# Splitting the weights on the engine that subtracts, and loading two of them through a second staging tile

## The chip, the cores and the metric

The kernel runs as one program on all 8 cores of one Trainium2 chip. Each core takes its own 4096 tokens with 256 tokens of warm-up in front (4352 tokens, 17 tiles of 256); there is no traffic between cores. The metric is device time in microseconds (us) of the slowest core.

## The reference

One layer of a "sandwich": a gated linear attention and a gated feed-forward network, each between two layer norms and added to its input.

```python
x = x + LN(attn(LN(x)));  x = x + LN(ffn(LN(x)))      # x: (2, 16384, 1024) f32
# attn: q = silu(x Wq^T); f = sigmoid(x Wk^T); g = log_sigmoid(f); k = 1 - f; v = x Wv^T
#       S = exp(g_t) S + k_t v_t^T ; o_t = q_t S (8 heads of 128) ; out = rmsnorm(o) * norm_w @ Wo^T
# ffn:  xr, xk = mixes of x and its predecessor in time by mu_r, mu_k
#       out = sigmoid(xr Wr^T) * (relu(xk Wk2^T)^2 Wv2^T)
```

## The kernel before

Activations lie transposed: 1024 features as 8 groups of 128 partitions, 256 tokens along the free dimension, so a tile is 128 x 2048 f32. Every f32 operand of a large product is split into a bf16 high part and a bf16 rest (`_h`, `_l`), and each product is three bf16 matmuls (high·high, high·rest, rest·high) added up in PSUM. `proj_feature` (L241) does this for one group of 128 output features: 24 matmuls into one of the two banks `p_pj`, after which another engine must empty the bank before the next but one group starts.

Phase A (before L690) holds Wk, Wq and Wv split in SBUF, runs the attention for 17 tiles and stores its result in the DRAM tensor `o_scr`. Phase B then takes the same SBUF for Wo, Wr, Wk2 and Wv2 and runs, tile by tile, the output projection and the feed-forward part.

Each weight comes in through `load_split_weight` (L166): 8 rounds, one for each 128 rows. In a round SP issues a 512 KB DMA into the one staging tile `wstage` (L172), ScalarE (ACT) copies it to bf16 (L180), and VectorE (DVE) or GpSimd (POOL) subtracts that high part from the f32 value into the rest (L183). The next DMA waits for the subtraction, as there is one staging tile; Wo has a scaling by `norm_w` on DVE ahead of the copy (L176). So nothing overlaps within a weight, and the weights of a phase follow each other.

The order between the phases is that of the program text, engine by engine: the DMAs of tile 0 (`b_load_dma`), Wo's rounds, then tile 0's output projection (`b_load_wo`), its scaling (`b_aobc`), its residual (`b_x2`, which puts the load of the next `xB` into SP's queue, waiting for DVE), and its second norm and mixes (`b_ln2_xrxk`). Only then come the rounds of Wr, Wk2 and Wv2, then the DMA of `oB` for tile 1. Each loop turn `it` from 1 to 17 then does, for p = `it` and q = p - 1: `b_load_wo(p)`, `b_wr(q)`, `b_wk2(q)`, `b_wv2(q)`, `b_aobc(p)`, `b_ffstat(q)`, `b_fin(q)`, `b_x2(p)`, `b_ln2_xrxk(p)`. In `b_load_wo` ACT copies `oB` to the high part `o_h` (L759), POOL subtracts (L761), TensorE (PE) multiplies, and ACT empties each bank into `scr1` (L768); the first of these copies waits until the mixes of the tile before (`pv["xk"]`, DVE L935) have read `scr1`. The mixes of `b_ln2_xrxk` are a chain of DVE instructions from L912 to L935 that uses `scr2` from L921 on.

Each `bld.flush()` closes a block of instructions on every engine; there is one after each loop turn and between the stages above. ACT works with function tables; the instruction ACT_TABLE_LOAD is put in by the compiler and bears the line of the instruction behind it.

Of the kernel before, what the change touches and what calls it, by code (L numbers as in the profile page):

```python
# [8 lines left out]
AF = mybir.ActivationFunctionType  # L9
ALU = mybir.AluOpType  # L10

D = 1024
# [80 lines left out]
def build_program(tok, warm, debug=False):  # L93
# [30 lines left out]
    op, ev, C = bld.op, bld.ev, bld.cnt  # L124
# [30 lines left out]
    for dst, src in ((mask4, mask4v), (onesc, onescv), (onesr, onesrv),  # L155
                     (nw, nwv), (mur, murv), (muk, mukv)):
        op("sync", lambda e, dst=dst, src=src: e.dma_start(out=dst[:], in_=src),
           inc=[("LW", 16)])
# [4 lines left out]
    op("vector", lambda e: e.memset(eps5[:], EPS_LN), inc=[("V", 1)], nop=True)  # L163
    op("vector", lambda e: e.memset(eps6[:], EPS_RMS), inc=[("V", 1)], nop=True)

    def load_split_weight(src_ap, dst_h, dst_l, scale_nw=False, first_wait=(), eng="vector"):  # L166
        E = "V" if eng == "vector" else "G"
        srcc = src_ap.rearrange("(c p) n -> p c n", p=128)
        last = None
        for ci in range(NCH):  # L170
            wv = [(E, C[E])] + (list(first_wait) if ci == 0 else [])
            op("sync", lambda e, ci=ci, srcc=srcc: e.dma_start(  # L172
                out=wstage[:], in_=srcc[:, ci:ci + 1, :]), wait=wv, inc=[("LW", 16)])
            wl = [("LW", C["LW"]), ev_cdma]
            if scale_nw:
                op(eng, lambda e, ci=ci: e.tensor_scalar_mul(  # L176
                    wstage[:, 0, :], wstage[:, 0, :], nw[:, ci:ci + 1]),
                   wait=wl + [(E, C[E])], inc=[(E, 1)])
                wl = [(E, C[E])]
            ev_h = op("scalar", lambda e, dst_h=dst_h, ci=ci: e.activation(  # L180
                out=dst_h[:, ci, :], in_=wstage[:, 0, :], func=AF.Copy),
                wait=wl + [("S", C["S"])], inc=[("S", 1)])
            op(eng, lambda e, dst_h=dst_h, dst_l=dst_l, ci=ci: e.tensor_tensor(  # L183
                dst_l[:, ci:ci + 1, :], wstage[:], dst_h[:, ci:ci + 1, :], ALU.subtract),
               wait=[ev_h, (E, C[E])], inc=[(E, 1)])
            last = ev(E)
        return last

    state = {
        "bc_read": ("V", 0),  # L190
        "bc_ev": ("T", 0),
        "pj_free": [("V", 0), ("V", 0)],
        "stats_free": ("V", 0),
# [64 lines left out]
    for nm in ("wk", "wq", "wv"):  # L258
# [27 lines left out]
    Ax_h = ctxA.enter_context(nc.sbuf_tensor("Ax_h", [128, 2, 512], BF16))  # L286
    Ax_l = ctxA.enter_context(nc.sbuf_tensor("Ax_l", [128, 2, 512], BF16))

    ev_wk = load_split_weight(w_in["wkT"], wA["wkh"], wA["wkl"], eng="vector")
    ev_wq = load_split_weight(w_in["wqT"], wA["wqh"], wA["wql"], first_wait=[ev_wk],  # L290
                              eng="gpsimd")
    ev_wv = load_split_weight(w_in["wvT"], wA["wvh"], wA["wvl"], first_wait=[ev_wq],
                              eng="vector")
    bld.flush()

    st = {
# [454 lines left out]
    def b_load_wo(p):  # L751
        pv = bt[p - 1] if p > 0 else bt[nt]
        me = bt[p]
        if p > 0:
            b_load_dma(p)
        ev_o = ev("LO")
        ev_rrow = ev("LR")
        me["x_ld"] = ("LX", C["LX"])
        ev_oh = op("scalar", lambda e: e.activation(out=o_h, in_=oB[:], func=AF.Copy),  # L759
                   wait=[ev_o, pv["WoT"], pv["revac"], ("S", C["S"])], inc=[("S", 1)])  # L760
        op("gpsimd", lambda e: e.tensor_tensor(o_l, oB[:], o_h, ALU.subtract),  # L761
           wait=[ev_oh, ("G", C["G"])], inc=[("G", 1)])
        ev_ospl = ev("G")
        ev_aoev = None
        for dj in range(NCH):
            evt = proj_feature(wB["woh"], wB["wol"], o_h, o_l, dj,
                               extra_wait=[ev_ospl, ev_wo] if dj < 2 else [])
            ev_aoev = op("scalar", lambda e, dj=dj: e.activation(  # L768
                out=scr1[:, dj, :], in_=p_pj[dj % 2][:, 0:TILE], func=AF.Copy),
                wait=[evt, pv["xk"], ("S", C["S"])], inc=[("S", 1)])  # L770
            state["pj_free"][dj % 2] = ev_aoev
        me["WoT"] = ("T", C["T"])
        ev_sq = op("scalar", lambda e: e.activation(out=sqA, in_=scr1[:], func=AF.Square),
                   wait=[ev_aoev, ("LO", C["LO"]), state["stats_free"], ("S", C["S"])],
                   inc=[("S", 1)])
# [25 lines left out]

    def b_wk2(q):
        me = bt[q]
        ev_kev = None
        for dj in range(NCH):
            evt = proj_feature(wB["wk2h"], wB["wk2l"], xk_h, xk_l, dj,
                               extra_wait=[ev_wk2, me["xk"]] if dj < 2 else [])
            ev_kev = op("scalar", lambda e, dj=dj: e.activation(
                out=scr2[:, dj, :], in_=p_pj[dj % 2][:, 0:TILE], func=AF.Relu),
                wait=[evt, bt[q - 1]["ffstat"] if q > 0 else TZ, ("S", C["S"])]  # L810
                if dj == 0 else [evt],
                inc=[("S", 1)])
            state["pj_free"][dj % 2] = ev_kev
        ev_wk2T = ("T", C["T"])
        op("vector", lambda e: e.tensor_tensor(scr2[:], scr2[:], scr2[:], ALU.mult),
           wait=[ev_kev, ("V", C["V"])], inc=[("V", 1)])
        op("vector", lambda e: e.tensor_copy(kc_h[:], scr2[:]),
           wait=[("V", C["V"]), ev_wk2T], inc=[("V", 1)])
        op("vector", lambda e: e.tensor_tensor(kc_l[:], scr2[:], kc_h[:], ALU.subtract),  # L819
           wait=[("V", C["V"])], inc=[("V", 1)])  # L820
        me["kc"] = ev("V")
# [16 lines left out]
    def b_aobc(p):  # L838
        me = bt[p]
        bcast_rows()  # L840
        me["aobc"] = ("T", C["T"])
        op("vector", lambda e: e.tensor_tensor(scr1[:], scr1[:], bcA(), ALU.mult),
           wait=[me["aobc"], ("V", C["V"])], inc=[("V", 1)])
        op("vector", lambda e: e.tensor_tensor(scr1[:], scr1[:], bcB(), ALU.add),
           wait=[("V", C["V"])], inc=[("V", 1)])
        state["bc_read"] = ev("V")
# [44 lines left out]
    def b_ln2_xrxk(p):  # L891
# [23 lines left out]
        mur_bc = mur[:].unsqueeze(2).broadcast_to([128, NCH, TILE])  # L915
        muk_bc = muk[:].unsqueeze(2).broadcast_to([128, NCH, TILE])
        q = p - 1
        gate_scr2 = bt[q]["ffstat"] if q >= 0 else TZ
        gate_xr = bt[q]["WrT"] if q >= 0 else TZ
        gate_xk = bt[q]["Wv2T"] if q >= 0 else TZ  # L920
        op("vector", lambda e: e.tensor_tensor(scr2[:], scr1[:], mur_bc, ALU.mult),  # L921
# [14 lines left out]
           wait=[("V", C["V"])], inc=[("V", 1)])  # L936
        me["xk"] = ev("V")

    b_load_dma(0)
    ev_wo = load_split_weight(w_in["woT"], wB["woh"], wB["wol"], scale_nw=True,  # L940
                              first_wait=ev_A_drain, eng="vector")
    op("vector", lambda e: e.memset(ln2[:], 0.0), inc=[("V", 1)], nop=True)
    ev_ln2init = ev("V")
    b_load_wo(0)
    b_aobc(0)
    b_x2(0)
    b_ln2_xrxk(0)
    bld.flush()
    ev_wr = load_split_weight(w_in["wrT"], wB["wrh"], wB["wrl"], first_wait=[ev_wo],
                              eng="gpsimd")  # L950
    ev_wk2 = load_split_weight(w_in["wk2T"], wB["wk2h"], wB["wk2l"], first_wait=[ev_wr],
                               eng="vector")
    ev_wv2 = load_split_weight(w_in["wv2T"], wB["wv2h"], wB["wv2l"], first_wait=[ev_wk2],
                               eng="gpsimd")
    bld.flush()
    for it in range(1, nt + 1):
        p, q = it, it - 1
# [94 lines left out]
```

How the kernel before makes its waits and increments, by code:

```python
        def closure(e, fn=fn, waits=waits, incs=tuple(incs), nop=nop):  # L51
            for sem, v in waits:
                e.wait_ge(sem, v)
            if nop:
                e.engine_nop()
            ins = fn(e)
            for sem, k in incs:
                ins.then_inc(sem, k)
# [11 lines left out]
        def closure(e, waits=waits):  # L70
            for sem, v in waits:
                e.wait_ge(sem, v)
```

## Time and profile before

| | us |
|---|---|
| profiled execution, time | 5739.41 |
| profiled execution, span of the slowest core | 5737.9 |
| runs shown | 5741.77 and 6156.08, median 5948.93 |

| engine | busy us | share of the span |
|---|---|---|
| PE | 3483.3 | 61% |
| DVE | 1945.3 | 34% |
| ACT | 1153.0 | 20% |
| POOL | 478.6 | 8% |

The profile is one execution, taken on the slowest core. "Busy" is the time in instructions of an engine. A wait is shown as idle time ahead of an instruction with what released it. The chain that ended last is followed back from the last instruction, at each step to what released it. Of that chain 52% is PE, 27% DVE, 9% ACT, 5% DMA, 4% issue and 2% POOL.

### The profile page before, as it was taken

Reading aid. Unit: us, or ns where it says so; the run is one execution under the profiler, and the core shown is the slowest. Engines: PE = TensorE matmul, PEld = TensorE weight load, DVE = VectorE, ACT = ScalarE, POOL = GpSimd, SP = SyncE. Lnnn points to the kernel's source line nnn. Section 1 sums busy time; section 2 is a strip of 40 time slices with the busy share of each in tenths; the row PEclk is TensorE's granted clock in tenths of the full one; section 3 lists DMA queues with packets and bytes.
Section 4 is the critical chain, followed back from the end, with each engine's and each line's share of the span. In section 5 each row is a group of like instructions: output and inputs, shape, how many; then the busy total and the mean of one; then the engine's idle time right before and its main releaser. Section 6 shows DMA issues by size and latency. Waiting matters only on the chain.

```text
span 5737.9 us, 65929 instructions; the slowest of 8 cores (5727.0 to 5737.9 us)
## 1 busy us (share of the span) xinstructions
PE 3483.3 (61%) x26608; PEld 2616.6 (46%) x26608; DVE 1945.3 (34%) x1912; ACT 1153.0 (20%) x1672; POOL 478.6 (8%) x198
## 2 busy tenths in 40 slices
PE   0566666666666666662236666766566675656675
PEld 0344444444444444441134455544445554444554
DVE  1333333333333333333303323333433323333233
ACT  1222222222222222222111111111111111111110
POOL 1111111111111111111110000000000000000000
PEclk9877777777777777776667888878788887878887
DMA  2000000000000000001110000000000000000000
GB/s 78 26 15 15 15 15 15 15 15 15 15 15 16 15 15 15 15 8 52 52 52 15 23 23 8 15 23 23 23 23 23 8 16 23 23 23 23 23 8 8
DMA packets 69041, 121.85 MB, mean 21 GB/s; under 512 B 3683, under 2 KB 55046, under 8 KB 62214
## 3 DMA queue, kind: packets, MB, share of 16 engines
q1 hardware_dynamic: 68742, 117.63, 6.2%
q8 instruction: 216, 3.54, 0.3%
q14 instruction: 83, 0.68, 0.0%
HBM read 83.00 MB, written 34.62 MB: 20 GB/s over the span
## 4 chain that ended last, share of the span: by engine, by line
PE 52%; DVE 27%; ACT 9%; DMA 5%; issue 4%; POOL 2%; DVEq 1%; ACTq 0%; SPq 0%; POOLq 0%
PE p_pj L250 38%; PE p_st L231 4%; PE p_pj L402 4%; DVE b_sb L331 3%; DVE r_a L207 1%; PE p_O L516 1%; PE p_O L533 1%; DMA outT<-x_sb 1%; ACT ebq L363 1%; PE p_A L481 1%; PE p_bc L216 1%; DVE p_A L459 1%; DVE scr L912 1%; DVE A_l L464 1%; DVE A_h L462 1%
## 5 line engine op out<-in xcount | busy, mean ns | idle before, releaser
L250 PE MATMUL p_pj<-o_pair,woh 128*128 128x256 bf16 x2176 | 419.5, 300 | 516.8 <-POOL o_pair L761 333.3
L250 PEld LDWEIGHTS p_pj<-o_pair,woh 128*128 128x128 bf16 x2176 | 230.9, 107 | 576.6 <-issue 531.8
L231 PE MATMUL p_st<-x_sb,onesc 128*1 128x256 f32 x544 | 179.7, 503 | 485.9 <-ACT oB L894 275.6
L250 PE MATMUL p_pj<-ln_h,wkh 128*128 128x256 bf16 x1088 | 308.3, 283 | 199.6 <-DVE ln_l L614 199.6
L250 PE MATMUL p_pj<-xk_h,wv2h 128*128 128x256 bf16 x1088 | 311.2, 286 | 119.0 <-DVE xk_l L819 119.0
L231 PEld LDWEIGHTS p_st<-x_sb,onesc 128*1 128x1 f32 x544 | 54.6, 103 | 610.1 <-issue 584.2
L250 PE MATMUL p_pj<-o_pair,wol 128*128 128x256 bf16 x1088 | 325.0, 299 | 0.0
L250 PE MATMUL p_pj<-xr_h,wrh 128*128 128x256 bf16 x1088 | 297.6, 274 | 25.0 <-DVE xk_l L935 24.8
L250 PE MATMUL p_pj<-xk_l,wv2h 128*128 128x256 bf16 x1088 | 311.6, 286 | 0.0
L250 PE MATMUL p_pj<-ln_h,wqh 128*128 128x256 bf16 x1088 | 310.1, 285 | 2.5 <-ACT fq_sb L649 2.5
L250 PE MATMUL p_pj<-xk_h,wv2l 128*128 128x256 bf16 x1088 | 310.3, 285 | 0.0
L250 PE MATMUL p_pj<-ln_l,wqh 128*128 128x256 bf16 x1088 | 309.2, 284 | 0.0
L250 PE MATMUL p_pj<-ln_h,wql 128*128 128x256 bf16 x1088 | 308.8, 284 | 0.0
L250 PE MATMUL p_pj<-ln_l,wkh 128*128 128x256 bf16 x1088 | 308.8, 284 | 0.0
L250 PE MATMUL p_pj<-ln_h,wkl 128*128 128x256 bf16 x1088 | 307.7, 283 | 0.0
L250 PE MATMUL p_pj<-xr_l,wrh 128*128 128x256 bf16 x1088 | 297.5, 273 | 0.0
L250 PE MATMUL p_pj<-xr_h,wrl 128*128 128x256 bf16 x1088 | 297.5, 273 | 0.0
L250 PE MATMUL p_pj<-xk_l,wk2h 128*128 128x256 bf16 x1088 | 296.6, 273 | 0.0
L250 PE MATMUL p_pj<-xk_h,wk2l 128*128 128x256 bf16 x1088 | 296.6, 273 | 0.0
L250 PE MATMUL p_pj<-xk_h,wk2h 128*128 128x256 bf16 x1088 | 296.6, 273 | 0.0
L481 PE MATMUL p_A<-qt_h,kx_h 128*128 128x128 bf16 x264 | 71.5, 280 | 369.3 <-DVE A_l L464 369.3
L761 POOL TENSOR_TENSOR o_pair<-oB,o_pair 128x2048 bf16<-128x2048 f32 x17 | 69.1, 4065 | 2544.3 <-ACT o_pair L759 2544.3
(177 smaller groups left out, 7936.7 us busy)
## 6 DMA issues: line engine op xcount, KB each, us to landing
x_sb<-xT SPq DMA_DIRECT2D x17, 1024.0 KB, 5.0
o_scr<-o_stage SPq DMA_DIRECT2D x68, 256.0 KB, 2.3
oB<-o_scr SPq DMA_DIRECT2D x17, 1024.0 KB, 4.9
xB<-xT SPq DMA_DIRECT2D x17, 1024.0 KB, 5.0
outT<-x_sb SPq DMA_DIRECT2D x16, 1024.0 KB, 4.4
wstage<-wkT SPq DMA_DIRECT2D x8, 512.0 KB
wstage<-wqT SPq DMA_DIRECT2D x8, 512.0 KB
wstage<-wvT SPq DMA_DIRECT2D x8, 512.0 KB
```

The lines of the kernel that those rows point to most:

```text
L207: op("vector", lambda e: e.reciprocal(r_a[:], r_t0[:]), wait=[("S", C["S"])], inc=[("V", 1)], nop=True)
L216: op("tensor", lambda e: e.matmul(p_bc[:, 0:TILE], onesr[:], r_a[:], start=True, stop=False), wait=wv)
L231: op("tensor", lambda e, ci=ci: e.matmul(p_st[0:1, 0:TILE], onesc[:], x_ap[:, ci, :], start=(ci == 0), stop=(ci == NCH - 1)), wait=wv if c ...
L250: e.matmul(bank[:, 0:TILE], wop[:, ci, dj * 128:(dj + 1) * 128], xop[:, ci, :], start=first, stop=last),
L331: op("vector", lambda e, h=h, tsl=tsl: e.tensor_tensor_scan(b_sb[:, h, :], g_sb[:, h, tsl], g_sb[:, h, tsl], 0.0, ALU.add, ALU.bypass), wa ...
L363: op("scalar", lambda e, h=h: e.activation(out=ebq[:, h, :], in_=b_sb[:, h, :], func=AF.Exp, scale=-1.0, bias=b_sb[:, h, CH - 1:CH]), wait ...
L402: e.matmul(bank[:], lnop[:, ci, tsl], wop[:, ci, half * 512:(half + 1) * 512], start=first, stop=last),
L459: op("vector", lambda e, bank=bank: e.tensor_tensor(bank[:], bank[:], mask4[:], ALU.mult), wait=[ev_Amm[g4], ("V", C["V"])], inc=[("V", 1)])
L462: op("vector", lambda e, bank=bank, Ah=Ah: e.tensor_copy(Ah[:], bank[:]), wait=[("V", C["V"])], inc=[("V", 1)])
L464: op("vector", lambda e, bank=bank, Ah=Ah, Al=Al: e.tensor_tensor(Al[:], bank[:], Ah[:], ALU.subtract), wait=[("V", C["V"])], inc=[("V", 1)])
L481: e.matmul(bank[:, (h - 4 * g4) * 128:(h - 4 * g4 + 1) * 128], kop[:, xpar, h, :], qop[:, h, :], start=first, stop=last),
L761: op("gpsimd", lambda e: e.tensor_tensor(o_l, oB[:], o_h, ALU.subtract), wait=[ev_oh, ("G", C["G"])], inc=[("G", 1)])
```

## The change

`load_split_weight` lets DVE or POOL itself make the bf16 copy that ACT made, and gets a staging tile and a semaphore as arguments. Wr and Wv2 are staged in the first half of `scr2` instead of `wstage`, split by POOL, and their 16 rounds stand ahead of tile 0's `b_aobc`, `b_x2` and `b_ln2_xrxk` in the program; the users of `scr2` wait for them (`scr2_ld`). Wk2 stays behind tile 0's mixes, through `wstage`, split by DVE. In `b_load_wo` the copy to `o_h` moves from ACT to POOL, for all 17 tiles.

```diff
@@ load_split_weight(..., stage=None, lsem="LW")
+        wst = wstage[:] if stage is None else stage
-            op("sync", ... dma_start(out=wstage[:], ...), wait=wv, inc=[("LW", 16)])
+            op("sync", ... dma_start(out=wst, ...), wait=wv, inc=[(lsem, 16)])
-            ev_h = op("scalar", lambda e, dst_h=dst_h, ci=ci: e.activation(
-                out=dst_h[:, ci, :], in_=wstage[:, 0, :], func=AF.Copy),
-                wait=wl + [("S", C["S"])], inc=[("S", 1)])
-            op(eng, ... e.tensor_tensor(
-                dst_l[:, ci:ci + 1, :], wstage[:], dst_h[:, ci:ci + 1, :], ALU.subtract),
-               wait=[ev_h, (E, C[E])], inc=[(E, 1)])
+            op(eng, lambda e, dst_h=dst_h, ci=ci, wst=wst: e.tensor_copy(
+                dst_h[:, ci:ci + 1, :], wst), wait=wl + [(E, C[E])], inc=[(E, 1)])
+            op(eng, ... e.tensor_tensor(
+                dst_l[:, ci:ci + 1, :], wst, dst_h[:, ci:ci + 1, :], ALU.subtract),
+               wait=[(E, C[E])], inc=[(E, 1)])
@@ b_load_wo
-        ev_oh = op("scalar", lambda e: e.activation(out=o_h, in_=oB[:], func=AF.Copy),
-                   wait=[ev_o, pv["WoT"], pv["revac"], ("S", C["S"])], inc=[("S", 1)])
+        op("gpsimd", lambda e: e.tensor_copy(o_h, oB[:]),
+           wait=[ev_o, pv["WoT"], pv["revac"], ("G", C["G"])], inc=[("G", 1)])
         op("gpsimd", lambda e: e.tensor_tensor(o_l, oB[:], o_h, ALU.subtract),
-           wait=[ev_oh, ("G", C["G"])], inc=[("G", 1)])
+           wait=[("G", C["G"])], inc=[("G", 1)])
@@ b_wk2, b_ln2_xrxk (tile 0's first writer of scr2)
-   ... else TZ
+   ... else state["scr2_ld"]
@@ between the phases
+    sview = scr2[:].rearrange("p a b -> p (a b)")[:, 0:D].unsqueeze(1)
     b_load_dma(0)
     ev_wo = load_split_weight(w_in["woT"], ..., scale_nw=True,
-                              first_wait=ev_A_drain, eng="vector")
+                              first_wait=ev_A_drain, eng="vector", lsem="SW")
     ...
     b_load_wo(0)
+    ev_wr = load_split_weight(w_in["wrT"], ..., first_wait=ev_A_drain,
+                              eng="gpsimd", stage=sview, lsem="LB")
+    ev_wv2 = load_split_weight(w_in["wv2T"], ..., first_wait=[ev_wr],
+                               eng="gpsimd", stage=sview, lsem="LB")
+    state["scr2_ld"] = ev_wv2
     b_aobc(0)
     b_x2(0)
     b_ln2_xrxk(0)
     bld.flush()
-    ev_wr = load_split_weight(..., first_wait=[ev_wo], eng="gpsimd")
-    ev_wk2 = load_split_weight(..., first_wait=[ev_wr], eng="vector")
-    ev_wv2 = load_split_weight(..., first_wait=[ev_wk2], eng="gpsimd")
+    ev_wk2 = load_split_weight(w_in["wk2T"], ..., first_wait=[ev_wo],
+                               eng="vector", lsem="SW")
```

Wk, Wq and Wv keep their order and `wstage`; their loads count on another semaphore.

## Rows read from the trace of the kernel before

**Rows 1.** Busy by windows, weight stretch: us, PE, PEld, DVE, ACT, POOL, PEclk, DMA, GB/s.
```profile
2800.00:2957.00 157.00, 0.00 (x0) 0.00 (x0) 27.43 (x16) 26.43 (x24) 36.41 (x15) 0.50 0.25 79
```

**Rows 2.** Chain that ended last, first weights: start us, length us, what.
```profile
16.25 1.06 ACT wkh L180
17.48 1.24 DVE wkl L183
...
22.50 1.06 ACT wkh L180
...
66.93 1.06 ACT wqh L180
68.19 2.13 POOL wql L183
...
74.12 1.06 ACT wqh L180
```

**Rows 3.** The same chain between the two phases.
```profile
2717.22 3.51 DMA wstage<-woT
...
2942.45 6.84 DMA oB<-o_scr
...
2957.17 23.24 PE p_pj L250 x192
```

**Rows 4.** Timeline of SP's queue between the phases: start, length, what.
```profile
2774.79 61.43 SPq L172 DMA_DIRECT2D wstage<-wrT  x8
2842.85 43.48 SPq L172 DMA_DIRECT2D wstage<-wk2T  x8
2892.54 49.71 SPq L172 DMA_DIRECT2D wstage<-wv2T  x8
```

**Rows 5.** Groups by line and shape: xcount | busy us, mean ns | idle before.
```profile
L183 DVE TENSOR_TENSOR wkl<-wstage,wkh 128x1024 bf16<-128x1024 f32 x8 | 9.8, 1225 | 44.9 <-ACT wkh L180 44.9
...
L817 DVE CAST xk_h<-scr 128x2048 bf16<-128x2048 f32 x17 | 20.8, 1226 | 2.9 <-DVE scr L815 2.9
...
L912 DVE TENSOR_TENSOR scr<-ln 128x2048 f32<-128x2048 f32 x17 | 52.0, 3060 | 1.8
...
L638 POOL TENSOR_SCALAR k_sb<-fq_sb 128x2048 f32<-128x2048 f32 x17 | 32.3, 1898 | 999.5 <-ACT fq_sb L627 999.5
...
L761 POOL TENSOR_TENSOR o_pair<-oB,o_pair 128x2048 bf16<-128x2048 f32 x17 | 69.1, 4065 | 2544.3 <-ACT o_pair L759 2544.3
```

**Rows 6.** The same view, ACT's table loads.
```profile
L759 ACT ACT_TABLE_LOAD x16 | 20.5, 1283 | 44.3 <-DMA oB<-o_scr 44.3
...
L180 ACT ACT_TABLE_LOAD x3 | 3.8, 1283 | 22.4 <-DVE wstage L176 13.5 <-DMA wstage<-wkT 8.8
```

**Rows 7.** Timeline of one later tile: POOL, then DVE, then ACT.
```profile
3436.05 4.07 POOL L761 TENSOR_TENSOR o_pair<-oB,o_pair 128x2048 bf16<-128x2048 f32 x1 [163.38 <-ACT o_pair L759]
...
3438.99 3.27 DVE L912 TENSOR_TENSOR scr<-ln 128x2048 f32<-128x2048 f32 x1
3442.51 2.29 DVE L921 TENSOR_TENSOR scr<-scr,mur 128x2048 f32<-128x2048 f32 x1 [0.24 <-DVE scr L912]
...
3457.29 2.29 DVE L935 TENSOR_TENSOR xk_l<-scr,xk_h 128x2048 bf16<-128x2048 f32 x1
...
3432.64 1.28 ACT L759 ACT_TABLE_LOAD   x1 [2.91 <-DMA oB<-o_scr]
...
3459.73 0.86 ACT L768 ACTIVATE scr<-p_pj 128x256 f32<-128x256 f32 x2 [23.88 <-DVE xk_l L935]
```

**Rows 8.** ACT's timeline around a table load.
```profile
3321.20 0.51 ACT L789 ACTIVATE r_msq<-r_var,eps 1x256 f32<-1x256 f32 x1 [8.25 <-DVE r_var L787]
3321.78 1.28 ACT L728 ACT_TABLE_LOAD   x1
3323.07 0.38 ACT L728 ACTIVATE r_sb<-p_pj 128x256 f32<-128x256 f32 x1
```

**Rows 9.** Waits, whole span: us in total, times, longest.
```profile
PE p_pj L250 <- ACT scr L768: 183.5, 15, 13.3
```

More of the change, by code:

```diff
@@ L164, in build_program, with load_split_weight @@
     op("vector", lambda e: e.memset(eps6[:], EPS_RMS), inc=[("V", 1)], nop=True)
-    def load_split_weight(src_ap, dst_h, dst_l, scale_nw=False, first_wait=(), eng="vector"):
+    def load_split_weight(src_ap, dst_h, dst_l, scale_nw=False, first_wait=(), eng="vector",
+                          stage=None, lsem="LW"):
         E = "V" if eng == "vector" else "G"
+        wst = wstage[:] if stage is None else stage
         srcc = src_ap.rearrange("(c p) n -> p c n", p=128)
@@ L171, in load_split_weight @@
             wv = [(E, C[E])] + (list(first_wait) if ci == 0 else [])
-            op("sync", lambda e, ci=ci, srcc=srcc: e.dma_start(
-                out=wstage[:], in_=srcc[:, ci:ci + 1, :]), wait=wv, inc=[("LW", 16)])
-            wl = [("LW", C["LW"]), ev_cdma]
+            op("sync", lambda e, ci=ci, srcc=srcc, wst=wst: e.dma_start(
+                out=wst, in_=srcc[:, ci:ci + 1, :]), wait=wv, inc=[(lsem, 16)])
+            wl = [(lsem, C[lsem]), ev_cdma]
             if scale_nw:
-                op(eng, lambda e, ci=ci: e.tensor_scalar_mul(
-                    wstage[:, 0, :], wstage[:, 0, :], nw[:, ci:ci + 1]),
+                op(eng, lambda e, ci=ci, wst=wst: e.tensor_scalar_mul(
+                    wst[:, 0, :], wst[:, 0, :], nw[:, ci:ci + 1]),
                    wait=wl + [(E, C[E])], inc=[(E, 1)])
                 wl = [(E, C[E])]
-            ev_h = op("scalar", lambda e, dst_h=dst_h, ci=ci: e.activation(
-                out=dst_h[:, ci, :], in_=wstage[:, 0, :], func=AF.Copy),
-                wait=wl + [("S", C["S"])], inc=[("S", 1)])
-            op(eng, lambda e, dst_h=dst_h, dst_l=dst_l, ci=ci: e.tensor_tensor(
-                dst_l[:, ci:ci + 1, :], wstage[:], dst_h[:, ci:ci + 1, :], ALU.subtract),
-               wait=[ev_h, (E, C[E])], inc=[(E, 1)])
+            op(eng, lambda e, dst_h=dst_h, ci=ci, wst=wst: e.tensor_copy(
+                dst_h[:, ci:ci + 1, :], wst), wait=wl + [(E, C[E])], inc=[(E, 1)])
+            op(eng, lambda e, dst_h=dst_h, dst_l=dst_l, ci=ci, wst=wst: e.tensor_tensor(
+                dst_l[:, ci:ci + 1, :], wst, dst_h[:, ci:ci + 1, :], ALU.subtract),
+               wait=[(E, C[E])], inc=[(E, 1)])
             last = ev(E)
@@ L190, in build_program @@
         "bc_read": ("V", 0),
+        "scr2_ld": ("G", 0),
         "bc_ev": ("T", 0),
@@ L287, in build_program @@
     Ax_l = ctxA.enter_context(nc.sbuf_tensor("Ax_l", [128, 2, 512], BF16))
-    ev_wk = load_split_weight(w_in["wkT"], wA["wkh"], wA["wkl"], eng="vector")
+    ev_wk = load_split_weight(w_in["wkT"], wA["wkh"], wA["wkl"], eng="vector",
+                              lsem="TT")
     ev_wq = load_split_weight(w_in["wqT"], wA["wqh"], wA["wql"], first_wait=[ev_wk],
-                              eng="gpsimd")
+                              eng="gpsimd", lsem="TT")
     ev_wv = load_split_weight(w_in["wvT"], wA["wvh"], wA["wvl"], first_wait=[ev_wq],
-                              eng="vector")
+                              eng="vector", lsem="TT")
     bld.flush()
@@ L809, in b_wk2 @@
                 out=scr2[:, dj, :], in_=p_pj[dj % 2][:, 0:TILE], func=AF.Relu),
-                wait=[evt, bt[q - 1]["ffstat"] if q > 0 else TZ, ("S", C["S"])]
+                wait=[evt, bt[q - 1]["ffstat"] if q > 0 else state["scr2_ld"],
+                      ("S", C["S"])]
                 if dj == 0 else [evt],
@@ L917, in b_ln2_xrxk @@
         q = p - 1
-        gate_scr2 = bt[q]["ffstat"] if q >= 0 else TZ
+        gate_scr2 = bt[q]["ffstat"] if q >= 0 else state["scr2_ld"]
         gate_xr = bt[q]["WrT"] if q >= 0 else TZ
@@ L944, in build_program @@
     b_load_wo(0)
+    ev_wr = load_split_weight(w_in["wrT"], wB["wrh"], wB["wrl"], first_wait=ev_A_drain,
+                              eng="gpsimd", stage=sview, lsem="LB")
+    ev_wv2 = load_split_weight(w_in["wv2T"], wB["wv2h"], wB["wv2l"], first_wait=[ev_wr],
+                               eng="gpsimd", stage=sview, lsem="LB")
+    state["scr2_ld"] = ev_wv2
     b_aobc(0)
@@ L948, in build_program @@
     bld.flush()
[L949 to L954, printed above, removed]
+    ev_wk2 = load_split_weight(w_in["wk2T"], wB["wk2h"], wB["wk2l"], first_wait=[ev_wo],
+                               eng="vector", lsem="SW")
     bld.flush()
```

## The prediction, made before the changed kernel was seen

> **What bounds the kernel now.** I read the busy shares of the page first (PE is highest at 61%, so waits matter), then the chain that ended last, then the windows in which PE does nothing. PE stands still in two stretches: the first 157 us, and the one between the phases, where in 157 us it has no instruction at all and its granted clock is 0.50 [rows 1]. Both are weight loads. The chain shows a round's structure: copy on ACT, subtraction, DMA, copy, one after the other. From copy to copy a DVE round is 22.50 - 16.25 = 6.25 us and a POOL round 74.12 - 66.93 = 7.19 us [rows 2]. SP's queue gives the same for the later weights: seven periods of Wk2 in 43.48 - 0.33 (the last issue) is 6.16 us each, Wv2 7.05, and Wr 8.73, since tile 0's DVE chain runs beside it [rows 4]. PE starts tile 1 at 2957.17, at the end of wv2's last round, then oB's DMA, ACT's copy and POOL's subtraction [rows 3]. In the later tiles the end is set by a serial loop in which the DVE mixes count: ACT's first copy out of PSUM waits for L935 and PE waits for ACT [rows 7], in 15 tiles [rows 9].
>
> **A round.** On DVE the ACT copy and its hand-over (17.48 - 16.25 = 1.23 us [rows 2]) give way to a DVE copy of 128x1024. That form isn't in the trace; the subtraction at 1024 takes 1.23 and at 2048 2.29 [rows 5, 7], so about 0.16 is fixed, and the copy of 2048 with 1.23 [rows 5] gives 0.16 + 1.07/2 = 0.69, at most the subtraction's 1.23. With a hand-over of 0.10 that is 0.79: 0.44 saved in each round. On POOL 1.26 us (68.19 - 66.93 [rows 2]) give way to a POOL copy. The nearest rows are one-input POOL work on 2048 (L638, 1.90) and the two-input subtraction (4.07 for 2048 [rows 5], 2.13 for 1024 [rows 2]), fixed part about 0.18. Half of L638's rest is 0.86 + 0.18 = 1.04 as the likely value, since the copy reads one input as L638 does; the dear end is 2.13, the cheap end the DVE's 0.69. With a hand-over of 0.15 a POOL round goes from 7.19 to 7.12: nothing gained. The Trainium skill (GPSIMD Engine Reference, Engine selection) puts one-input GpSimd work at roughly line rate and two-input work at about twice the DVE's time; the two rows agree with both.
>
> **The first weights.** Wk and Wv: 16 x 0.44 = 7.0. Wq: 8 x 0.07 = 0.6. ACT's first table load of 1.28 [rows 6] goes from the path: DVE starts at once. Together -8.9 us, with no cover over it, since nothing else runs.
>
> **Between the phases.** In the times of before, without those 8.9 us:
> - Wo's eighth issue was at 2717.22 [rows 3]. It comes 1.28 (table load, one of the three at L180 [rows 6]) and 7 x 0.44 = 3.1 earlier, and about 2 later, because POOL now splits tile 0's oB while Wo's first rounds need DVE: 2714.8. That POOL and DVE get in each other's way is in the trace: L912 takes 3.27 instead of 2.29 where POOL's L761 is still running, and its end at 3442.26 is POOL's end 3440.12 plus nearly its own 2.29 [rows 7].
> - PE's Wo(0) now follows Wo's last subtraction directly, as oB was split meanwhile. That chain no longer sets the end: tile 0's mixes will wait at L921 for scr2.
> - Wr's first DMA is issued 0.5 later in SP's queue (its waits, POOL's split and the drain of phase A, are over) and lands after 3.5 plus 1 for sharing with Wo's: 2719.8. Sixteen POOL rounds: the first 3.3 without its DMA, fifteen of 7.12 are 106.8: 2829.9. Collisions with DVE cost Wr's seven periods 61.43 - 49.71 = 11.7 us [rows 4] under the whole chain of mixes; now only x2 and L912 and small row work meet them: +3, so 2833.
> - Behind Wv2 waits DVE's L921, and behind it the mixes: from 3442.51 to 3459.58 is 17.1 us [rows 7]: 2850. Wk2's DMAs wait for their end; xB's load stands ahead of them in SP's queue but was released long before. Seven periods of 6.16 - 0.44 = 5.72 are 40.0: eighth issue 2890. oB's DMA follows 0.5 later and lands after 6.84 [rows 3]: 2897.5. POOL copy 1.90 and subtraction 4.07 with hand-overs of 0.5: PE starts tile 1 at 2904, where it was 2957.2. That is -53 us.
>
> **The later tiles.** ACT loses L759, which isn't on the path: PE does two groups after it and then stands until 3459.73, so an earlier Wo start is worth nothing. Two things around it count.
> - POOL starts about where ACT's table load started, 3432.64 [rows 7]: + 0.1 + 1.90 + 0.15 + 4.07 = 3438.86, just before L912 at 3438.99. L912's excess is 52.0 - 17 x 2.29 = 13.1 us over all tiles [rows 5]: -12. With a POOL copy at 4.07 it would be 15 x 1.1 = 16 dearer instead.
> - The table load doesn't vanish. ACT loads one in each of the 16 turns that begin with L759 [rows 6], after the wait of that instruction (the DMA), also with Sqrt already done before, while L789's Sqrt behind the Copy needs none: each block of instructions begins without a known table. L759 was the first ACT instruction of its block; now it is L768, whose wait is for L935. So a load of 1.28 that lay under other work moves between DVE's mixes and PE: 15 x 1.28 = +19.2 us. In tiles 0 and 1 L768 waits for PE only, and PE has the other bank to fill: nothing.
>
> Around a load I count no more than its 1.28: L789 ends at 3321.71, the load begins at 3321.78 and the next ACTIVATE at 3323.07 [rows 8]. The Trainium skill (ScalarE: Activation LUTs, What ACT_TABLE_LOAD costs) adds a drain of about 1.38 us to each switch; by that page the move would cost 40 us and the estimate would end near 5705. No drain shows in the row.
>
> **Sum.** -8.9 - 53 - 12 + 19.2 = -54.7. The profiled execution took 5739.4 us, 0.04% below the lower of the two runs shown and 3.5% below their median, which lies between two far values. The forecast goes by the profiled execution: 5739.4 - 54.7 = 5684.7, taken as 5684.
>
> **The rivals.**
> 1. *The table load isn't exposed*: the compiler needs none ahead of the Copy, or puts it ahead of the wait. For it: only L768's place in a block is inferred. Against: all 16 loads of L759 come right behind its DMA wait. Then 5684 - 19 = 5665. The Trainium skill (ScalarE: Activation LUTs, Table sets) says that cheap functions are in every set, which speaks for this one; the load at L759, itself a Copy, speaks against it. Chance 0.13.
> 2. *The POOL copy costs as much as the subtraction*, 2.13 and 4.07. For it: nothing but that the form is unseen. Then 24 rounds on the path x 1.09 = 26, tile 1's split 2, and in the later tiles 16 + 12 = 28 more: 5740, no change. Chance 0.13.
> 3. *Slower than before*: a POOL copy of more than 2.1 us for 1024 elements per partition. From there each further us costs 24 for the weight rounds and 15 x 2 = 30 in L912's wait: at 3.1 us it is 5794, within 2% still. Against it is L638. Chance 0.03.
> 4. *The rounds between the phases overlap better or worse*: no collisions and a full cover give 5 us less, collisions as Wr had over all of tile 0's work 9 more, and a DVE copy without its double speed 32 x 0.54 = 17 more: 5679 to 5710. This is the range of the forecast itself, whose chance is 0.68. The last 0.03 is for what I don't see.
>
> So the likeliest case's own range is 5672 to 5710; with the rivals, 8 times in 10 it is 5660 to 5725. A measurement tells about 2% (115 us) from no change; all cases but the tails lie within it: faster 0.03, same 0.95, slower 0.02.
>
> **What would show it.** Right: weight rounds of 5.8 on DVE and 7.1 on POOL; a POOL copy of 1.9 at L759's place; L912 at 2.29; PE's first matmul of tile 1 about 62 us earlier (2895); a table load at L768 in 16 turns, in 15 of them between L935 and the copy. Wrong: a POOL copy above 1.5 for 1024, no load at L768, or PE starting tile 1 later than 2910, which would mean that the sixteen POOL rounds collide more than 3 us' worth.

## The result, and the profile after

The changed kernel is faster by 1.1%: the ratio of the times is 0.9894, with an interval of 0.9877 to 0.991. In microseconds that is 61 of 5740. Its profiled execution took 5669.09 us where that of before took 5739.41, so 70.3 less, and the forecast was 54.7 less. The other times of the changed kernel in the comparison go from 5668.4 to 5691.8, those of before from 5740.2 to 5741.8; the profiled execution lies near the low end of its own. In some executions of every kernel the cores of a die ran at a lower clock and longer; all times, stages and ratios below are of undisturbed executions or dies.

The cores of the changed kernel, with the granted clock:

```profile
die 0 (median of its cores): 5664.0 us, clock 0.806
die 1 (median of its cores): 5662.7 us, clock 0.806
```

To see where time went I cut each core's trace at four marks: SP's issue of the first `x_sb`, the first and the last store of `rms_scr` (one in each turn of phase A), and PE's first matmul of tile 1 in phase B. These are medians over the cores, in us; the last column is the core's whole span. Short labels are those of the experiments.

```
kernel        x_sb issued  to 1st store  loop A  between  loop B  core span
before            156.6        200.8     2299.2   297.8   2778.0   5731.8
after             149.8        199.9     2288.5   243.8   2782.1   5663.0
e1_copies         149.4        200.1     2291.9   285.7   2777.0   5705.8
e2_order          157.9        200.1     2285.6   311.6   2777.5   5735.7
e3_oh             157.0        201.8     2299.2   292.9   2786.8   5738.9
e4_delay1         164.2        200.1     2293.7   298.8   2781.0   5737.6
e6_hide           150.4        201.4     2285.1   243.4   2778.1   5659.9
e7_delay          157.7        199.9     2287.0   244.0   2786.2   5677.5
e9_oh_back        150.9        201.1     2286.8   246.2   2777.8   5663.6
e10_one           157.2        201.7     2298.9   298.2   2777.6   5734.1
e11_two           158.0        200.8     2299.2   297.1   2778.1   5733.7
e12_three         158.2        199.8     2299.2   297.1   2778.7   5732.8
```

In e7_delay cores 2 and 3 ran at a lower clock (0.801 beside 0.804 to 0.806) and their loop B took 2801 to 2802; its die 1 alone has 2784.0 there.

So -6.8 for the first weights, -54.0 between the phases, -10.7 in a loop whose code is the same, and +4.1 in loop B.

The chain that ended last, between the phases of the changed kernel (start, length, what), answers [rows 3]:

```profile
2641.54 8.47 DMA wstage<-woT
2650.24 2.86 DVE wstage L178
...
2696.62 4.15 DMA scr<-wrT
2702.24 2.93 POOL wrl L184
...
2813.18 2.30 DVE scr L925
...
2830.18 3.86 DMA wstage<-wk2T
...
2873.25 5.44 DMA oB<-o_scr
2880.97 4.07 POOL o_pair L764
2885.27 23.94 PE p_pj L252 x192
```

And SP's queue for the same stretch, to be held against [rows 4]:

```profile
2696.62 52.12 SPq L174 DMA_DIRECT2D scr<-wrT  x8
2755.45 50.95 SPq L174 DMA_DIRECT2D scr<-wv2T  x8
2806.51 0.37 SPq L892 DMA_DIRECT2D xB<-xT  x1
2830.18 42.87 SPq L174 DMA_DIRECT2D wstage<-wk2T  x8
2873.25 0.33 SPq L745 DMA_DIRECT2D oB<-o_scr  x1
```

The reader is to see the chain that was forecast. Sixteen POOL rounds follow each other without a hole, DVE's first mix on `scr2` starts as the last of them ends, Wk2 follows the mixes, then `oB`. PE starts tile 1 at 2885.27 instead of 2957.17, 71.9 earlier. The forecast of that point was 62 earlier; on these two cores 18.4 of the 71.9 are there before the last store of phase A's loop (7.7 from the start, 10.7 in the loop), and about 53.5 are gained between the phases.

The groups by line and shape, to be held against [rows 5]:

```profile
L182 DVE CAST wkh<-wstage 128x1024 bf16<-128x1024 f32 x8 | 5.6, 694 | 34.2 <-DMA wstage<-wkT 34.2
L182 POOL CAST wqh<-wstage 128x1024 bf16<-128x1024 f32 x8 | 8.3, 1036 | 81.7 <-DMA wstage<-wqT 81.7
L762 POOL CAST o_pair<-oB 128x2048 bf16<-128x2048 f32 x17 | 32.1, 1890 | 2518.3 <-DMA oB<-o_scr 2518.3
L916 DVE TENSOR_TENSOR scr<-ln 128x2048 f32<-128x2048 f32 x17 | 39.0, 2292 | 1.8
L771 ACT ACT_TABLE_LOAD x17 | 21.8, 1283 | 638.7 <-DVE xk_l L939 440.1 <-PE p_pj L252 198.7
```

The forms that no row of before showed were bounded well: 0.694 us against 0.69 worked out for DVE, 1.036 against 1.04 and 1.890 against 1.90 for POOL. L916 (L912 before) is down from 3060 to 2292 ns, and the table load now stands at L771 (L768 before), 17 times, 15 of them behind DVE's `xk_l` and 2 behind PE.

One later tile, POOL, DVE and ACT, answers [rows 7], and the two waits answer [rows 9]:

```profile
3363.87 4.07 POOL L764 TENSOR_TENSOR o_pair<-oB,o_pair 128x2048 bf16<-128x2048 f32 x1
3368.34 2.29 DVE L916 TENSOR_TENSOR scr<-ln 128x2048 f32<-128x2048 f32 x1
3386.02 2.29 DVE L939 TENSOR_TENSOR xk_l<-scr,xk_h 128x2048 bf16<-128x2048 f32 x1
3388.45 1.28 ACT L771 ACT_TABLE_LOAD   x1 [29.27 <-DVE xk_l L939]
3389.74 0.86 ACT L771 ACTIVATE scr<-p_pj 128x256 f32<-128x256 f32 x2
```

```profile
ACT L771 <- DVE xk_l L939: 440.1, 15, 29.6
PE p_pj L252 <- ACT scr L771: 220.0, 15, 14.9
```

POOL is done (3367.94) before L916 starts, so L916 is undisturbed. Then `xk_l` ends at 3388.31, the load runs its 1.28, and the copy starts at 3389.74. PE's wait behind these copies rose from 183.5 to 220.0, 2.4 us in each of the 15 tiles; that is more than the load alone, and the section on the table load comes back to it. Both mechanisms of the later tiles are there. No drain shows on top of the load, so here the trace departs from the Trainium skill (ScalarE: Activation LUTs, What ACT_TABLE_LOAD costs), as the prediction had it.

### The profile page after: what moved, and what is told of

Read it like the earlier page. It is cut to its first block, busy times and chain, and to the rows that moved or that the text cites. A ratio compares the mean times of both kernels' runs of the same rounds, so it can differ in the third digit from the quotient of the medians.

```text
span 5667.5 us, 65908 instructions; the slowest of 8 cores (5657.1 to 5667.5 us)
## 1 busy us (share of the span) xinstructions
PE 3463.3 (61%) x26608; PEld 2611.2 (46%) x26608; DVE 1955.6 (35%) x1944; ACT 1059.6 (19%) x1597; POOL 532.0 (9%) x239
## 4 chain that ended last, share of the span: by engine, by line
PE 52%; DVE 27%; ACT 7%; DMA 5%; issue 5%; POOL 3%; DVEq 1%; ACTq 0%; POOLq 0%; SPq 0%
PE p_pj L252 39%; PE p_pj L405 4%; PE p_st L233 4%; DVE b_sb L334 3%; PE p_O L519 1%; DVE r_a L209 1%; PE p_O L536 1%; DMA outT<-x_sb 1%; ACT ebq L366 1%; DVE qt_h L348 1%; DVE p_A L462 1%; PE p_A L484 1%; DVE A_l L467 1%; DVE A_h L465 1%; ACT xsq_bf L557 1%
## 5 line engine op out<-in xcount | busy, mean ns | idle before, releaser
L762 POOL CAST o_pair<-oB 128x2048 bf16<-128x2048 f32 x17 | 32.1, 1890 | 2518.3 <-DMA oB<-o_scr 2518.3
```

## Experiments: the parts of the change alone

Beside these runs before gave no time near its 5740 (the lowest is 5771.9), so no ratio is given for them; the stages of the traces are compared.

**The copies alone.** Before, with the weights' copies on DVE and POOL, in the old order; `o_h` stays on ACT.

```diff
-            ev_h = op("scalar", lambda e, ...: e.activation(out=dst_h[:, ci, :], in_=wstage[:, 0, :], func=AF.Copy), ...)
+            op(eng, lambda e, ...: e.tensor_copy(dst_h[:, ci:ci + 1, :], wstage[:]), wait=wl + [(E, C[E])], inc=[(E, 1)])
```

> The kernel before with one part of the change: DVE or POOL makes the bf16 copies of all seven weights; order, staging tile and the o_h copy on ACT stay. Baseline is 5740.5 us. Theory 'sum' (each us taken off the path comes off the end, attention turns as in the kernel before): first weights -8, between the phases 16 DVE rounds x 0.44, 16 POOL rounds x 0.07 and two table loads of 1.28, -10.7, together 5721 to 5723; phase A's loop from its first to its last rms_scr store stays at 2299 us on most cores, all turns 146.7 to 147.1. Theory 'clock' (an attention turn also depends on when PE's granted clock comes back to full, and that on when the loop starts): the loop starts about as in the changed kernel, so it shows the same 143.3 and 144.8 us turns there, 2285 to 2289 us, and the total is 5708 to 5714.

Measured: 7.2 us off the first weights, 12.1 off the stretch between the phases, loop A 7.3 shorter, loop B as before; times 5715.4 and 5720.1. The two stretches agree with the round arithmetic (-8 and -10.7) within 1.4 us. Loop A agrees with neither theory: 'sum' left it at 2299, 'clock' put it at 2285 to 2289, and it took 2291.9, so that the times lie between the two totals too.

**The order alone.** Before, with the staging of Wr and Wv2 in `scr2` and their rounds ahead of tile 0's mixes, but all copies still on ACT.

```diff
+    ev_wr = load_split_weight(w_in["wrT"], ..., first_wait=ev_A_drain, eng="gpsimd", stage=sview, lsem="LB")
+    ev_wv2 = load_split_weight(w_in["wv2T"], ..., first_wait=[ev_wr], eng="gpsimd", stage=sview, lsem="LB")
     b_aobc(0)
     b_x2(0)
     b_ln2_xrxk(0)
```

> The kernel before with the other part: Wr and Wv2 staged in scr2 ahead of tile 0's mixes, but all bf16 copies stay on ACT, o_h too. ACT empties Wo(0)'s banks ahead of the first Wr copy in its queue, so the sixteen rounds can start only behind its Sqrt of tile 0, some 45 us later than in the changed kernel. Theory 'the order alone brings the gain': between the phases -45 or better, total about 5690. Theory 'the order needs the copies off ACT': rounds of Wr start at about 2762, sixteen of 7.19 end near 2874, the mixes end at 2892, Wk2's eight rounds at 2941, PE starts tile 1 at about 2950 instead of 2957: total 5733, range 5725 to 5741. The attention turns are those of the kernel before, 2299 us.

Measured: the stretch between the phases grew by 13.8 us; the lowest time is 5746.8. Both theories had a gain there, 45 us or about 7; both missed. So did the expectation for phase A's loop: it took 2285.6 and not 2299, although everything that this edit reorders stands behind it. ACT's timeline of this kernel on core 4 shows why the stretch between the phases grew:

```profile
2743.51 0.51 ACT L793 ACTIVATE r_msq<-r_var,eps 1x256 f32<-1x256 f32 x1 [6.58 <-DVE r_var L791]
2744.10 1.06 ACT L182 ACTIVATE wrh<-scr 128x1024 bf16<-128x1024 f32 x1
...
2851.72 1.06 ACT L182 ACTIVATE wv2h<-scr 128x1024 bf16<-128x1024 f32 x1 [6.47 <-DMA scr<-wv2T]
2852.87 1.91 ACT L899 ACTIVATE oB<-x_sb 128x2048 bf16<-128x2048 f32 x1
```

ACT takes its queue in order. The sixteen copies of Wr and Wv2 stand behind tile 0's output projection (L772 to L793), so Wr starts only at 2744, and ahead of tile 0's Square (L899), so tile 0's norm and mixes start only after them. The overlap is lost on both sides. Moving the copies off ACT is therefore not only cheaper by a fraction of a microsecond in each round; it is what lets the order overlap at all. Copies alone give -12.1, order alone +13.8, both without the move of `o_h` -51.6 (e9_oh_back below), the whole change -54.0.

**`o_h` on POOL alone.** Before, with only the edit of `b_load_wo`.

```diff
-        ev_oh = op("scalar", lambda e: e.activation(out=o_h, in_=oB[:], func=AF.Copy), ...)
+        op("gpsimd", lambda e: e.tensor_copy(o_h, oB[:]), wait=[ev_o, pv["WoT"], pv["revac"], ("G", C["G"])], inc=[("G", 1)])
```

> The kernel before with o_h's copy on POOL only. Theory 'sum': in the later tiles L912 loses 12 us of waiting and 15 table loads of 1.28 come between L935 and L768, +7; tile 0's split is done early, -4, tile 1's -1.5: 5742. Theory 'clock': a turn of phase B is 167.2 us in both kernels whatever a fraction of a us in it does, so the +7 doesn't appear: 5735, turns of 167.2 with one or two of 170. Under both, L912 takes 2.29 and the trace shows the table load at L768 behind L935.

Measured: -4.9 between the phases and +8.8 in loop B; the lowest time is 5743.7. The number is near the +7.2 of the sum for the later tiles, but by luck: its turns don't grow by 0.5 each. Most are 167.2 to 167.6, as before, and on each core two to four of them are 170.0 to 170.3, three us longer. The expectation's other theory, turns that keep their length, was right on the turns and wrong on how few would be long.

## Experiments: the exposed table load

**The changed kernel with the load hidden.** A 1x1 Sqrt without a wait on anything late, at the head of each tile in ACT's queue, whose result nothing reads. It takes the table load early.

```diff
+        op("scalar", lambda e: e.activation(out=act_dm[:], in_=eps5[:], func=AF.Sqrt, bias=eps5[:, 0:1]),
+           wait=[("S", C["S"])], inc=[("S", 1)])
         op("gpsimd", lambda e: e.tensor_copy(o_h, oB[:]), ...)
```

> The changed kernel with one 1x1 Sqrt on ACT put in b_load_wo ahead of everything ACT does there, its result unused: it takes the table load of the block early, while ACT is idle, so that L771's Copy finds its table loaded. Loop B (from PE's first matmul of tile 1 to the end) is 2782.1 us in the changed kernel, median of the cores. Theory 'sum': the 15 exposed loads of 1.28 go, loop B 2763, total 19 less than the changed kernel. Theory 'clock': turns of phase B keep the length of 167.2 us, only the few of 170.3 go; loop B 2776 to 2780, as in the kernel before, total 2 to 6 less. The load itself is seen to stand at the new line, under PE's statistics work, in both.

**The changed kernel with `o_h` back on ACT.**

```diff
-        op("gpsimd", lambda e: e.tensor_copy(o_h, oB[:]), ...)
+        ev_oh = op("scalar", lambda e: e.activation(out=o_h, in_=oB[:], func=AF.Copy), wait=[..., ("G", C["G"]), ("S", C["S"])], ...)
```

> The changed kernel with o_h's copy back on ACT, for all 17 tiles; weights as in the changed kernel. Theory 'the o_h move costs' (the run of the kernel before with that move alone gave loop B +8.8 us at the median of the cores and 4.9 less between the phases): loop B back from 2782 to 2777 or 2778, between the phases +1.5 for tile 1's table load and copy, total 3 us less than the changed kernel. Theory 'the o_h move pays' (L912's waits for POOL come back as 12 us): loop B 2790 or more. L912 is back at about 3.1 us in both.

Measured: the ratio to before is 0.9867 (0.9813 to 0.992) for the hidden load and 0.9869 (0.9828 to 0.991) with `o_h` back; neither can be told from the change's own 0.9894. Loop B is 4.0 and 4.3 us shorter than after, not the 19 that fifteen loads would make. With `o_h` back, L912's line (L916 here) takes 3100 ns again, with the load hidden it takes 2292, and the two loops B are equal (2777.8 and 2778.1): the 12 us at L912 don't reach the end either. The load did go; this is the group of the kernel with the early Sqrt:

```profile
L763 ACT ACT_TABLE_LOAD x17 | 21.8, 1283 | 1.6 <-ACT r_msq L207 0.4
```

Where do fifteen times 1.28 us go? I laid one turn of loop B of three kernels side by side, each from SP's issue of `oB` (lines are those of before; starts, but for L935, in us from that issue):

```
                                before core 6   after core 3   hidden load core 3
DVE L935 (xk_l) ends                32.05          31.34           31.15
ACT L768, first copy                32.20          32.77           31.30
ACT L768, last copy                 50.27          52.28           49.96
ACT L773 (square for the norm)      50.86          52.87           50.54
DVE L778 (mean, behind PE's sums)   58.34          58.72           58.08
DVE L815                           100.87         101.25          100.61
ACT L894                           159.68         159.60          159.38
next issue of oB                   167.26         167.26          167.25
```

At the first copy the changed kernel is 0.57 us behind before, which is the forecast's 1.28 - 0.8 = 0.48. By the last copy it is 2.0 behind. The added 1.4 goes with PE's clock: in the same 19 us of the turn (31 to 50 behind its start) the changed kernel's PE runs 127 matmuls at a mean granted clock of 0.78, that with the hidden load 144 at 0.87, before 144 at 0.88 (first the changed kernel; us, PE, PEld, DVE, ACT, POOL, PEclk, DMA, GB/s):

```profile
3387.97:3406.97 19.00, 16.70 (x127) 13.77 (x128) 0.34 (x1) 3.93 (x8) 0.00 (x0) 0.78 0.00 1
```

```profile
3393.11:3412.11 19.00, 17.93 (x144) 15.07 (x144) 0.15 (x1) 2.73 (x8) 0.00 (x0) 0.87 0.00 1
```

Then 1.6 of the 2.0 comes back between L773 and L778, and the rest by the end of the turn. What lies between L773 and L778 is PE's column sums. The same columns for 53 to 58 us behind the start of the turn, in which the sums lie, first the changed kernel, then the one with the hidden load:

```profile
3409.97:3414.97 5.00, 3.08 (x23) 1.27 (x24) 0.00 (x0) 1.77 (x1) 0.00 (x0) 1.00 0.00 0
```

```profile
3415.11:3420.11 5.00, 5.00 (x23) 1.61 (x22) 0.00 (x0) 0.00 (x0) 0.00 (x0) 0.66 0.00 0
```

23 of these matmuls take 3.08 us with the granted clock at 2.4 GHz, and fill all 5 us at a mean of 0.66, that is, mostly at 1.2 GHz (before: 0.68, all 5 us full). The kernel that begins its sums 2.3 us earlier has the clock lowered during them and loses 1.7 of it; the one that is late had its low clock already, under the copies, and sums at the high one. So the load is exposed and costs its 1.28 where it stands, and in this turn nothing of it is left at the end. This turn of loop B lasts 167.2 to 167.3 in all three. How the last few tenths are lost behind the sums, and whether something else also holds the turn at that length, these rows don't show. What remains is that one turn of the fifteen lasts 170.3 on every core of the changed kernel (two on core 0), where before has one on two of its eight cores and the kernel with the hidden load none.

## Experiments: why loop A is shorter

Phase A's loop has the same instructions in both kernels. Yet most of its turns last 146.7 to 147.1 or 143.1 to 144.8 us, and the changed kernel has more of the short ones (four to six of the fifteen full turns on a core, before none or one). Windows of 12.3 us at the same place of a turn, 73.3 us behind its start: in a short and in a long turn of the changed kernel, then in a long one of before (columns as above):

```profile
424.10:436.40 12.30, 9.66 (x67) 5.21 (x68) 1.23 (x2) 2.97 (x5) 0.00 (x0) 1.00 0.16 45
567.50:579.80 12.30, 9.01 (x54) 4.86 (x55) 1.23 (x2) 3.91 (x6) 0.00 (x0) 0.72 0.15 44
```

```profile
432.80:445.10 12.30, 9.88 (x53) 5.62 (x54) 1.23 (x2) 3.02 (x5) 0.00 (x0) 0.61 0.16 44
```

In the short turn (350.8 to 494.2) the granted clock is at 2.4 GHz throughout this stretch. In the long ones it is still low for a part of it. So what makes a turn short is where in it the clock comes back. What decides that? The first theory was the moment at which the loop starts, 7.7 us earlier after the change.

**Before, started later, and the changed kernel, started as late as before.** Both get a DVE memset ahead of the first `x_sb`, whose result is written over.

```diff
+    op("vector", lambda e: e.memset(g_sb[:, 0:5, :], 0.0), wait=[("V", C["V"])], inc=[("V", 1)])
+    st["x_free"] = ("V", C["V"])
     a_stats(0)
```

> The kernel before with one more DVE memset (128x1280 f32, about 1.1 us) between the first weights and the load of x_sb; its result is overwritten. Theory 'sum': +1.2 us, 5741.7, phase A's loop 2299.2 us on every core with turns of 146.7 to 147.1 as before. Theory 'clock': the loop's length changes by more than the delay in at least one turn (a turn of about 143.3 or 144.8 comes or goes), so that the loop isn't 2299.2 but 2285 to 2296 or 2302, and the total differs from 5740.5 by something else than 1.2, anywhere from -14 to +5.

> The changed kernel with one DVE memset (128x1280 f32) behind the last split of the first weights, and the load of x_sb waiting for it: x_sb is issued about 7 us later, at about 157, where it was in the kernel before. Theory 'sum': total +7, loop A stays 2288.5 as in the changed kernel. Theory 'clock by start': loop A's length follows the start, so it goes back to 2299, total +18. Theory 'clock, but not by the start alone' (the kernel before with the same edit, its x_sb 7.6 us later, had a loop A of 2290 to 2297 instead of 2299): some third length, 2285 to 2302, on different cores different ones.

Measured: the start moved by 7.6 and 7.9 us, more than I had meant in the first, since the issue now also waits for Wv's last split. Before's loop A became 2293.7 (between 2290 and 2297 on single cores). The changed kernel's stayed at 2287.0 although it started at 157.7; its ratio to before is 0.9919 (0.9879 to 0.9959). A changed kernel that starts as late as before keeps its short loop, so the start alone doesn't decide. The order alone says the same: start 157.9, loop A 2285.6.

**Before, with one, two and three tiny DMAs ahead of the first `x_sb`.**

```diff
+    op("sync", lambda e: e.dma_start(out=muk[:], in_=mukv), wait=[ev_cdma], inc=[("SX", 16)])
     a_stats(0)
```

> The kernel before with one more DMA issue of 4 KB (the constant muk once more) in SP's queue ahead of the first load of x_sb: x_sb and all of phase A behind it come about 0.45 us later, nothing else changes. Theory 'sum': loop A 2299.2 us as before, total +0.5. Theory 'clock': how PE's clock rises in a turn hangs on where the turn meets it; two traces differ by 0.27 us at one place of turn 1, and in one the clock rises 10 us sooner and the turn is 3.2 us shorter. So 0.45 us can be enough: loop A 2285 to 2296 on several cores, and the total falls although work was added, by 3 to 13.

> As the run with one more issue, but with two: x_sb 0.9 us later. 'Sum': loop A 2299.2, total +0.9. 'Clock': loop A 2285 to 2296 on several cores, or 2299 again; turns of 143 to 145 us in place of 146.8.

> As before, with three: x_sb 1.4 us later. 'Sum': loop A 2299.2, total +1.4. 'Clock': any of 2285 to 2299, and no steady course over the runs with one, two and three.

Measured: starts 0.6 to 1.6 us later, loop A 2299 in all three, with single cores of the first two at 2292 to 2296. The expectation that a small shift would make the loop fall into the short rhythm missed.

What holds: the loop's length comes in steps of about 3.4 us, and in the turns looked at the difference is where the clock comes back. Kernels with the loads of before on its semaphore and the copies on ACT gave 2299 (one of them 2294), those with the change's order 2285 to 2289, the copies alone 2292. A pair of turns of before and of the order alone ran alike until the clock rose 10 us apart, with PE's work only 0.27 us apart. What decides it stays open. One rival wasn't run: ahead of the loop the order alone differs from before only in the semaphore that the loads of Wk, Wq and Wv count on (and in the code that stands further on), and all kernels with that semaphore are among those of 2285 to 2289. Before with that semaphore alone would have been the next experiment.

## Experiments: a faster version

The stretches where PE stands still are set by one staging tile per queue: load, copy and subtraction in turn, so each round pays about 3.5 us of DMA. The next kernel keeps the change and lets the loads run ahead through a ring of staging tiles, in buffers that are idle then: five in phase A, four for Wo, Wr and Wk2 and two for Wv2 between the phases. ACT copies and DVE subtracts where tile 0 isn't running.

```diff
+    slA = [("Q0", wstage[:])] + list(zip(("Q1", "Q2", "Q3", "Q4"), halves(k_sb) + halves(g_sb)))
+    ev_wk, ev_wq, ev_wv = load_ring([(w_in["wkT"], ..., "A"), (w_in["wqT"], ..., "A"), (w_in["wvT"], ..., "A")], slA)
...
+    slV = list(zip(("Q0", "Q5", "Q1", "Q2"), [wstage[:], halves(scr2)[0]] + halves(x2_sb)))
+    slG = list(zip(("Q3", "Q4"), halves(r_sb)))
```

> A version built on the finding that a us taken from the weight stretches comes off the end one for one. Weights of phase A come through five staging tiles (wstage and the halves of k_sb and g_sb, free at that time), each with its own semaphore, copy on ACT and subtraction on DVE: the DMA latency of 3.5 us per round is then overlapped and a round costs 1.4 to 2.5 us instead of 5.8 to 7.1. Between the phases Wo (ACT and DVE), Wr and Wk2 (DVE) come through four staging tiles and Wv2 (POOL) through two more, all ahead of tile 0's mixes. o_h stays on POOL. If the latency was the cost: x_sb is issued at 50 to 65 us instead of 150, the stretch between the phases goes from 244 to 110 to 140, total 5440 to 5500. If all eight cores' loads meet a common limit at the DRAM (79 GB/s per core so far), rounds stay at 4 us or more and the total is 5550 or more. Loop B as in the changed kernel, 2782.

> The version with staged weights (core spans 5468 us at the median of undisturbed cores, x_sb issued at 44) with the early Sqrt on ACT that takes the table load from behind the mixes. In the changed kernel that edit took loop B from 2782 to 2778. If it adds to the staging: 5464, a gain of 4 over the version without it. If loop B is stepped by the clock from another start: 5455 to 5480, not to be told from it. First weights as there, x_sb at 44; stretch between the phases about 116 us.

The second is the first with the early Sqrt. Both change several things at once (the rings, the engine of each copy and subtraction, all four weights ahead of tile 0's mixes), so what the rings alone bring isn't separated. Measured: 0.9573 (0.951 to 0.9637) for the first, so 4.3% faster than before. The second took 5457.15 us in its profiled execution, beside 5739.5 for before on that chip (4.9% less); no interval can be given for it. Whether the early Sqrt adds anything to the rings can't be told from this one time. SP's queue of the second, core 4:

```profile
4.66 0.43 SPq L202 DMA_DIRECT2D k_sb<-wkT  x1
...
42.47 0.33 SPq L202 DMA_DIRECT2D g_sb<-wvT  x1
42.85 0.43 SPq L635 DMA_DIRECT2D x_sb<-xT  x1
...
2536.76 0.34 SPq L202 DMA_DIRECT2D wstage<-woT  x1
...
2601.06 29.23 SPq L202 DMA_DIRECT2D r_sb<-wv2T  x8
2632.42 0.33 SPq L935 DMA_DIRECT2D xB<-xT  x1
2639.51 0.33 SPq L785 DMA_DIRECT2D oB<-o_scr  x1
```

All 24 rounds of phase A are issued within 39 us (3.71 to 42.47), 1.7 each, where a round took 6 to 7. Between the phases 115 us pass from Wo's first issue to PE's first matmul of tile 1 (2651.89), where the changed kernel needs 243.7. So 105 and 129 us are gone from the two stretches, and the median core span fell by 214 (5663 to 5449). Most of the 20 missing from their sum is in the first turn of loop B, which lasts 163 to 169 us here (cores 4, 6 and 0) and 149 in the changed kernel (core 3).

## Why the prediction was right or wrong

Two steps failed. The first is the one from the sum to the verdict, "a measurement tells about 2% (115 us) from no change", which gave no change a chance of 0.95. The second is in the sum: phase A's loop, which stands at nothing in it, got 10.7 us shorter, and the +7.2 of the later tiles was carried to the end, where its parts don't show. The profiled 5669.09 lies below the likeliest case's own range of 5672 to 5710 and inside the wider 5660 to 5725. Over all times the gain is about 61 us, 6 more than the forecast's 54.7; the 15.6 by which the profiled execution is off is taken apart here.

- **"-8.9" for the first weights**: -7.7 on the profiled cores, -6.8 in the median. The table load did go: from the first issue of Wk to the second it was 8.84 us and is 7.22, 1.28 and 0.34 less. The six periods behind it gained 0.37 each and Wv's seven 0.48, where 0.44 was put; Wv's eighth round isn't ahead of the issue of `x_sb`, though the sum counted it. Wq's gained nothing where 0.6 was put in all: the 7.19 of one round [rows 2] was not the mean of its weight, whose periods were 7.12 before and 7.14 after.
- **"-53" between the phases**: -54.0. The chain holds, but the terms are up to 2.6 us off and cancel, so an agreement within 1 us is part luck. Wk2's seven periods took 42.6 where 40.0 was put, and `oB` landed after 5.4 where 6.8 was put. Wo's first scaling took 2.86 instead of 0.75 us behind POOL's split, 2.1 where "about 2" was taken. Wr's seven periods took 51.8 against Wv2's 50.6, so the collisions were 1.2 where "+3" was taken.
- **"-12" at L912**: L912's time fell by 13.0 us over all tiles, as forecast, and yet with that time back (e9_oh_back) loop B is no longer. **"15 x 1.28 = +19.2"**: the load is there, 15 times, at the place forecast. But the step that took their sum of +7.2 straight to the end is what failed. Loop B grew by 4.1, of which 3.1 is one longer turn; the other turns behind the first didn't change, and the last 1.0 isn't assigned. The chain through PE is right at the copies (+0.57); it left out that PE's granted clock moves with it. The kernel with late copies has its low clock under them (0.78 beside 0.87) and a high one in the sums, the one with early copies a low one there (1.00 beside 0.66). What makes a turn the longer one stays open.
- **Phase A's loop, taken as unchanged** with the same code: -10.7 us. This is the largest part missed, 10.7 of the 15.6 us between the forecast -54.7 and the measured -70.3. What sets it stays open, as the experiments show. The forecast assumed the same instructions take the same time. They don't to better than 0.5% here.
- **"A measurement tells about 2% (115 us) from no change; all cases but the tails lie within it"**: this is the step that made the verdict wrong. The comparison's interval is 0.33% wide, and a gain of 1.1% stands clear of no change. The times of before in it lie between 5740.2 and 5741.8, and the page could have told it: the profiled execution and the lower run shown were 0.04% apart. By its own sum of -54.7 us, nearly 1%, with a range of -14 to -79, the forecast should have read faster, with most of the chance. Its own lower end is not one number either: the fourth rival's terms give 5679, the range says 5672, and it doesn't say by which term.
- **The rivals.** "The table load isn't exposed" is refuted at the spot (3388.45), though its time of 5665 is the nearest to the 5669 measured: the right number for another reason. "The POOL copy costs as much as the subtraction" is refuted by 1036 ns, and with it the slower case. That the rounds "overlap better" came out 1 us better than the likely value, of the 5 allowed.

## What to carry to other kernels

Read a serial weight load by its rounds: with one staging tile each round pays the full landing of its DMA, about 3.5 us here. The version with five tiles there took 105 us off the first weights, where moving the copies took 7. Before interleaving two streams, look for every engine that both use in order; here ACT's copies had to go before the new order could pay. In a loop with PE pauses, a microsecond taken from or put on the path between two PE stretches may come back through the clock, so price it only where a measured turn changes. And judge what a measurement can tell by the spread of the repeated times (0.03% and 0.4% for the two kernels here), not by a round figure.

## What the runs showed of the hardware

- Unchanged code ran in 2285 to 2299 us (0.6%); in the turns looked at the difference is where the granted clock came back. Most turns of phase A last 146.7 to 147.1 or 143.1 to 144.8 us, and most of phase B 167.2 or, a few, 170.2.
- A table load of 1.283 us stands on ACT ahead of L759 or L771, the first ACT instruction of its block, though both are Copies, and it runs behind that instruction's wait: 15 times at L771 behind DVE. An early, tiny instruction without such a wait takes it away for 0.29 us of ACT's time.
- A DVE scaling of 128x1024 took 2.86 instead of 0.75 us while POOL's subtraction ran: it started at 2650.24 and ended at 2653.1, 0.56 behind POOL's end at 2652.54. In the 2.3 us in which both ran it did at most about 0.2 us of its work, so it stood still rather than shared. The Trainium skill (Advanced Engine Details and Errata, VectorE Performance Modes) has it that DVE instructions in a two-port mode and GpSimd ones block each other; the trace agrees with a block, though no run here shows which mode the scaling ran in.
